# A Swin block on one core: the MLP's rows turned by 32x32 blocks on VectorE and spread by 12 small transfers a unit, in place of TensorE transposes

## What is computed

```python
win = windows of 8x8 pixels of x rolled by (-4, -4)      # (4096, 64, 96)
h = layernorm(win, ln1)
q, k, v = h @ wq + bq, h @ wk + bk, h @ wv + bv          # 3 heads of 32
o = softmax(q k^T / sqrt(32)) v
win = win + o @ wo + bo
h2 = layernorm(win, ln2)
win = win + gelu(h2 @ w1 + b1) @ w2 + b2                 # 96 -> 384 -> 96
result = the windows put back and rolled by (4, 4)
```

## Time and profile before

| | |
|---|---|
| median of 3 runs | 5439.2 us (5439.17 to 5441.29) |
| the profiled execution, its own time | 5443.8 us |
| its span, first to last instruction | 5442.0 us |
| share of the span: PE, DVE, ACT, POOL busy | 95%, 77%, 69%, 57% |
| one batch, from one attention stretch's start to the next | 335 us |

### The profile page before, as it was taken

The page is one execution under the profiler, slowest core; times in us unless marked ns, Lnnn a source line. Parts: engine busy times, 40 slices in busy tenths (PEclk is TensorE's granted clock), DMA queues, the critical chain, the costliest instruction groups (busy, mean ns, idle before and its releaser), DMA issues.

```text
span 5442.0 us, 275140 instructions
## 1 busy us (share of the span) xinstructions
PE 5176.5 (95%) x105172; PEld 4395.4 (81%) x105172; DVE 4179.8 (77%) x9862; ACT 3741.6 (69%) x7758; POOL 3083.7 (57%) x3053
## 2 busy tenths in 40 slices
PE   6999999999999999999999999999999999999999
PEld 4887888878788787888878888788887888878888
DVE  6968768687686877869778697786977869688696
ACT  6839568495784957749477594875938659396693
POOL 5645646466464655646556466464664646556464
PEclk8999999999999999999999999999999999999999
DMA  3011020110201102010120201202011020110201
GB/s 98 3 44 48 27 68 6 47 42 27 68 9 51 36 30 65 11 57 27 33 62 15 61 19 36 59 16 66 13 38 57 19 70 6 41 54 22 73 3 44
DMA packets 92300, 213.96 MB, mean 39 GB/s; under 512 B 22058, under 2 KB 26379, under 8 KB 91851
## 3 DMA queue, kind: packets, MB, share of 16 engines
q1 hardware_dynamic: 91848, 208.20, 13.0%
q10 hardware_dynamic: 2, 0.00, 0.0%
HBM read 107.45 MB, written 100.66 MB: 38 GB/s over the span
## 4 chain that ended last, share of the span: by engine, by line
PE 88%; issue 5%; DVE 5%; SPq 1%; ACT 1%; POOL 0%; DVEq 0%; ACTq 0%; DMA 0%; POOLq 0%
PE psum L585 20%; PE psum L599 19%; PE psum L462 12%; PE psum L430 8%; PE psum L508 6%; PE psum L477 6%; PE psum L494 6%; PE psum L538 5%; PE psum L524 5%; DVE row_max L828 1%; DVE stats L807 1%; DVE stream L857 1%; SPq L251 1%; DVE probs L835 0%; DVE prob_sum L843 0%
## 5 line engine op out<-in xcount | busy, mean ns | idle before, releaser
L297 POOL TENSOR_TENSOR probs<-probs,prob_inv 128x512 f32<-128x512 f32 x771 | 783.1, 1044 | 1496.7 <-DVE prob_inv L851 1496.6
L857 DVE TENSOR_TENSOR stream<-stream,psum 128x384 f32 x1024 | 562.4, 553 | 850.3 <-PE psum L599 760.8
L736 ACT ACTIVATE gelu_odd<-psum 128x512 f32<-128x512 f32 x768 | 459.9, 599 | 732.7 <-PE psum L585 676.9
L736 ACT ACTIVATE gelu_even<-psum 128x512 f32<-128x512 f32 x768 | 459.6, 598 | 682.8 <-PE psum L585 627.1
L376 POOL TENSOR_TENSOR stream<-stream,b_all 128x768 f32 x256 | 493.2, 1931 | 612.4 <-DVE normed L877 584.8
L659 ACT ACTIVATE normed<-stream,shift,rstd 128x96 f32 (+1 forms) x2072 | 770.7, 461 | 43.9 <-POOL shift L345 23.2
L807 DVE BATCH_NORM_STATS2 stats<-stream (+2 forms) x4224 | 725.9, 243 | 57.1 <-DVE stream L857 38.9
L336 POOL TENSOR_TENSOR rstd<-variance,minus_half 128x32 f32<-128x32 f32 (+3 forms) x181 | 747.7, 4131 | 14.2
L304 POOL TENSOR_TENSOR hT<-hT_upper,hT_lower 96x1024 f32<-96x1024 f32 x258 | 613.6, 2378 | 22.8 <-issue 15.6
L828 DVE TENSOR_REDUCE row_max<-psum 128x8 f32<-128x512 f32 x771 | 523.8, 679 | 131.7 <-PE psum L494 116.6
L843 DVE TENSOR_REDUCE prob_sum<-probs 128x8 f32<-128x512 f32 x771 | 497.8, 679 | 109.1 <-ACT probs L693 109.1
(11 more groups left out here) (86 smaller groups left out, 10635.3 us busy)
## 6 DMA issues: line engine op xcount, KB each, us to landing
stream<-in_x SPq DMA_DIRECT2D x272, 192.0 KB
out<-stream SPq DMA_DIRECT2D x256, 192.0 KB
stream<-in_x SPq DMA_DIRECT2D x272, 180.0 KB
out<-stream SPq DMA_DIRECT2D x256, 180.0 KB
stream<-in_x SPq DMA_DIRECT2D x544, 6.0 KB
out<-stream SPq DMA_DIRECT2D x512, 6.0 KB
gelu_odd<-in_L_conv_w SPq DMA_DIRECT2D x1, 144.0 KB
w_w<-in_L_conv_w SPq DMA_DIRECT2D x1, 144.0 KB
```

The lines of the kernel that those rows point to most:

```text
L297: nc.gpsimd.tensor_tensor(block_h, block_h, inv, ALU.mult).then_inc(probs_ready, 1)
L736: nc.scalar.activation(gelu[parity][:, j, part * SHARES:(part + 1) * SHARES], psum[:, UP_BANKS[part][j], :], ACT.Gelu).then_inc(gelu_done, 1)
L857: nc.vector.tensor_tensor(part, part, psum[:, banks[g], 0:GROUP], ALU.add).then_inc(added, 1)
```

## The change

The MLP's h2 no longer goes through PE and PSUM.

- **Turning.** `turn_h2` on DVE transposes `normed2` by blocks of 32x32: 4 blocks of tokens x 3 blocks of channels for each of 8 tiles, in one instruction. Each block is turned where it lies, so it stays on its 32 partitions.
- **Spreading.** SP then moves the blocks to the partitions of their channels: 12 transfers a unit (`spread_h2`), each of 32 partitions x 256 values, 32 KB. They count on two semaphores, six transfers each.
- **Halves.** The upper half of `h2T` is made from the spread rows by ACT (`copy_h2T_upper`, two instructions of 96x512), for units 0 and 1 by DVE. The lower half is made by DVE as before, but from SBUF.
- **Buffers.** Turned rows of units 0 to 2 lie in a part of `gelu[1]`, the later ones in `normed1`; spread rows lie in `gelu[0]` (units 0, 1) and then alternately in `probsT` and `oT`, all idle at that time. There is one turned buffer for the units from 3 on: turning a unit waits until the unit before it has been spread.
- **Order of tokens.** Spread rows have the tokens of a tile in another order, so gelu writes its result through a view that puts them back.
- **Three units ahead.** Units 0, 1 and 2 of a batch are normalised by POOL in attention steps 4, 6 and 9, turned by DVE after steps 5, 8 and 11 and spread by SP; DVE makes the halves of units 0 and 1 after steps 6, 7, 9 and 10. Unit 2 is spread once attention of unit 15 has read `probsT`. `statistics1` moves from steps 8 to 10 to steps 2 to 4, and POOL has six `finish` calls in attention instead of four.
- **PE.** `transpose2` is gone. `down` waits for all six gelu tiles at once, where before each of its parts waited for three.

```diff
+            def spread_h2(u, source, raw, freed):
+                wait_apart(sp, h2_turned, u + 1)
+                if freed is not None:
+                    wait_apart(sp, *freed)
+                for tb in range(TBLOCKS):
+                    for cb in range(CBLOCKS):
+                        sp.dma_start(raw[BLOCK * cb:BLOCK * (cb + 1), RUN * tb:RUN * (tb + 1)],
+                                     source[BLOCK * tb:BLOCK * (tb + 1), RUN * cb:RUN * (cb + 1)])\
+                            .then_inc(h2_spread[tb // 2], 16)
+            def spread_late(u, parity):
+                spread_h2(u, turned_late, raw_late[parity], (h2T_copied, 2 * (u - 1)))
             def store_batch(batch_row):
-                with sp.Fori(0, BATCH_ROWS) as r:
+                batch = 2 * batch_row
+                spread_h2(batch, turned_early, raw_early[0], None)
+                spread_h2(batch + 1, turned_early, raw_early[1], None)
+                spread_h2(batch + 2, turned_early, raw_late[0], (pv_done, batch + BATCH))
+                with sp.Fori(0, 6) as r:
                     for half in (0, 1):
+                        spread_late(batch + 2 * r + half + 3, 1 - half)
                         store(batch_row + r, half)
+                spread_late(batch + BATCH - 1, 1)
...
-            def transpose2(u, steady):
-                pe.wait_ge(ln2_ready, u + 1)
-                if steady:
-                    pe.wait_ge(gelu_done, 2 * FCHUNKS * u - FCHUNKS)
-                for g in range(2):
-                    transpose_rows(normed2, T2_BANKS, g, t2_done)
...
+            def mlp_step(u, parity):
+                up(u, parity, 1, True)
+                up(u + 1, 1 - parity, 0, True)
+                down(u, parity, True)
...
+            def copy_h2T_upper(u, parity):
+                for g in range(2):
+                    tokens = slice(g * SHARES, (g + 1) * SHARES)
+                    act.wait_ge(h2_spread[g], 16 * SPREAD_DMAS * (u + 1))
+                    nc.scalar.activation(h2T[parity][0][0:C, tokens], raw_late[parity][:, tokens], ACT.Copy)\
+                        .then_inc(h2T_upper_done, 1)
...
+                gelus(batch, 0, 0)
+                with act.Fori(0, BATCH // 2 - 1) as k:
+                    for odd in (0, 1):
+                        j = 2 * k + odd
+                        gelus(batch + j, odd, 1)
+                        copy_h2T_upper(batch + j + 2, odd)
+                        gelus(batch + j + 1, 1 - odd, 0)
...
+            def turn_h2(u, turned, first):
+                dve.wait_ge(ln2_ready, u + 1)
+                if not first:
+                    for half in h2_spread:
+                        wait_apart(dve, half, 16 * SPREAD_DMAS * u)
+                nc.vector.transpose(turned.rearrange("p (b t i) -> p t b i", b=CBLOCKS, i=BLOCK),
+                                    normed2[:, :, :].rearrange("p t (b i) -> p t b i", i=BLOCK))\
+                    .then_inc(h2_turned, 1)
...
                 def mlp_step(j, parity, row, half):
-                    copy_h2T(batch + j + 1, 1 - parity)
-                    normalise2(batch + j + 2, j + 2)
-                    if row is not None:
-                        statistics1(batch + BATCH + AHEAD + j, AHEAD + j, batch_row + BATCH_ROWS + row, half)
-                    scale2(b, j + 2)
+                    normalise2(batch + j + 3, j + 3)
+                    scale2(b, batch + j + 3, j + 3)
+                    turn_h2(batch + j + 3, turned_late, False)
+                    statistics1(batch + BATCH + AHEAD + j, AHEAD + j, batch_row + BATCH_ROWS + row, half)
+                    copy_h2T_lower(batch + j + 2, parity, raw_late)
                     add_mlp(batch + j)
```

More of the change, by code:

```diff
@@ L589, in up, with down @@
                     last.then_inc(up_done, 1)
[L591 to L600, removed]
[L601 to L616 removed]
+            def down(u, parity, steady):
+                pe.wait_ge(gelu_done, 2 * FCHUNKS * (u + 1))
+                for part in range(2):
+                    if steady:
+                        pe.wait_ge(mlp_added, 2 * u + part)
+                    for t in range(TILES // 2):
+                        c = part * (TILES // 2) + t
+                        for j in range(FCHUNKS):
+                            for side in range(2):
+                                last = nc.tensor.matmul(
+                                    psum[WT * side:WT * (side + 1), DOWN_BANKS[part], t * C:(t + 1) * C],
+                                    gelu[parity][:, j, c * P + WT * side:c * P + WT * (side + 1)], w2_w[:, j, :],
+                                    start=(j == 0), stop=(j == FCHUNKS - 1))
+                    last.then_inc(down_done, 1)
+            def mlp_step(u, parity):
+                up(u, parity, 1, True)
+                up(u + 1, 1 - parity, 0, True)
+                down(u, parity, True)
             for u in range(-AHEAD, 0):
@@ L753, in _ @@
                 nc.scalar.preload_act_table_set("gelu_and_others")
-                with act.Fori(0, BATCH // 2) as k:
-                    for parity in (0, 1):
-                        gelus(batch + 2 * k + parity, parity, 0)
-                        gelus(batch + 2 * k + parity, parity, 1)
+                gelus(batch, 0, 0)
[5 more added lines that the diff above has]
+                        gelus(batch + j + 1, 1 - odd, 0)
+                gelus(batch + BATCH - 2, 0, 1)
+                gelus(batch + BATCH - 1, 1, 0)
+                gelus(batch + BATCH - 1, 1, 1)
         @block.vector
@@ L928, in _, with whole_step @@
                 batch = b * BATCH
-                with dve.Fori(0, 4) as r:
+                def whole_step(s):
+                    attention_step(batch + s, s % 2)
+                    statistics2(batch + s, s)
+                for s in range(2):
+                    whole_step(s)
+                for n in range(AHEAD):
+                    whole_step(2 + n)
+                    statistics1(batch + BATCH + n, n, batch_row + BATCH_ROWS + n // 2, n % 2)
+                whole_step(5)
+                turn_h2(batch, turned_early, True)
+                whole_step(6)
+                copy_h2T_upper(batch, 0)
+                whole_step(7)
+                copy_h2T_lower(batch, 0, raw_early)
+                whole_step(8)
+                turn_h2(batch + 1, turned_early, False)
+                whole_step(9)
+                copy_h2T_upper(batch + 1, 1)
+                whole_step(10)
+                copy_h2T_lower(batch + 1, 1, raw_early)
+                whole_step(11)
+                turn_h2(batch + 2, turned_early, False)
+                with dve.Fori(6, 8) as r:
                     for half in (0, 1):
```

153 lines of the change are left out of this document (78 added, 75 removed).

## The result

| | before | after |
|---|---|---|
| median of 4 runs, us | 5439.2 (5437.2 to 5441.3) | 5930.0 (5921.3 to 5934.8) |
| profiled execution, us (span) | 5443.8 (5442.0) | 5934.8 (5933.0) |
| mean granted clock of TensorE | 0.987 | 0.948 |
| from A to the end of the MLP stretch, mean of 16 | 150.4 | 176.1 |
| from there to the next A, mean of 15 | 185.2 | 190.3 |

After/before is 1.0901, 95% interval 1.0882 to 1.0919: 30.7 us more for each of the 16 batches. The last two lines are worked out from the ends of PE's last `project_out` product (A) and last `down` product of each batch: 25.7 us of the loss lie in the MLP stretch, 5.1 in attention.

What follows compares the result with a forecast made beforehand. PE was taken to bound the kernel, SP's queue the new MLP stretch: 151.05 - 135.2 = 15.85, minus 1.75 in attention, 14.1 us a batch, 226 in 16, giving 5213 us; range 5150 to 5400.

Steps and rivals of the forecast that it cites:

- Slower: Rival, chance 0.16: SP's issues cost what a store's do, I = 8.4, giving 5847 us; decides from a pitch of 0.515.
- I: SP's time to issue the 12 spreading transfers of one unit in the MLP stretch; forecast 5.1 us, ends 4.4 and 5.7.
- the price of an issue: SP's cost for each spreading transfer, taken as 0.415 us, the middle between two kinds of transfer in the earlier trace.
- the bound of 0.47: Upper end of the pitch of SP's 12 issues expected in the profile after, 0.36 to 0.47 us.
- start of unit 4's spreading: SP in the MLP stretch: unit 4 turned at A + 14.4, after add_mlp of unit 0, plus 0.2.
- eleven gaps between spreadings: SP's time between groups of 12 issues, units 4 to 15: six of 4.6 us and five of 2.8.
- Two units take 2I + 7.4, against PE's 16.5: MLP stretch: SP's loop over two units against two PE steps; the queue keeps pace up to I = 4.55 us.
- A + 74.0 + 12 I: End of the MLP stretch if SP's queue bounds; meets PE's A + 133.0 at I = 4.92, 135.2 us with 5.1.
- The PE-bound stretch: MLP stretch if PE bounds it: 133.0 us against 151.05, with steps of 8.24 us, a gain of 18.05 a batch.
- seven insertions: DVE's three turns, two upper and two lower pairs added in attention; forecast to cost 1.75 us a batch.
- the 0.3 us above: Cost to an attention step of one DVE insertion of 1.2 to 1.6 us, taken from steps holding statistics1.
- The bound of 8.1 us a batch: Attention: cost of DVE's added work if none of it is hidden, 3 x 0.97 + 4 x 1.3.

Runs made afterwards that it cites:

- cheap issues: Changed kernel with each of the 12 transfers reading its rows from the input in DRAM instead of the turned tile; output not the reference's; 5467.2 us, ratio 1.0045.
- through DRAM: Changed kernel with turned rows written to DRAM in one transfer and read back in three, early halves in mid-step; 5199.8 us, ratio 0.9550.
- both edits: Changed kernel with six double-size transfers a unit (rows misplaced) and the early halves in the middle of the next attention step; 5198.6 us, ratio 0.9557.
- repeated copies: Version with turned rows going by way of DRAM, each early upper copy made three times and each early lower half twice; 5285.4 us.
- six-issue version: Changed kernel with six transfers of twice the size a unit instead of 12, bytes unchanged, rows misplaced; 5286.0 us, ratio 0.9712.
- moved halves: Changed kernel with DVE's early halves of units 0 and 1 in the middle of the next attention step, behind three subtractions; 5845.7 us, ratio 1.0739.

## Why the prediction was wrong, point by point

It was wrong in sign, with 0.80 on faster. The rival *Slower* is what happened: the queue bounds, and the pitch, 0.633, is past the 0.515 from which it decides. Its reason was another than the one I gave for it: the spreading has no computed patterns, and the same transfers out of DRAM cost 0.42. That its 5847 us comes near 5930 is partly luck: it took I = 8.4, and with the measured 7.6 the same sum gives 74.0 + 91.2 = 165.2 for the stretch and 5693 us in all.

**The step that failed** is the price of an issue: "I take the middle, 0.415, so I = 12 x 0.415 + 0.1 for the wait = 5.1. Ends: 4.4 and 5.7". It interpolated over rows and bytes between rows that all had DRAM at one side; no row before showed a transfer with both sides in SBUF, and the bound of 0.47 did not hold for it. Measured: I = 7.6. Of the 12 x (7.6 - 5.1) = 30.0 us a batch that this costs, 12 x (7.6 - 5.5) = 25 are for both sides in SBUF (5.5 is I with DRAM at one side); the other 5 come from averaging in the pitch of 0.36, where a steady burst out of DRAM has 0.46.

The loss of 30.7 us a batch in place of a gain of 14.1 is a miss of 44.8. By terms, from the mean starts of the spreadings in 14 batches (unit 4 at A + 19.7, unit 15 at A + 148.8, end A + 176.1):

| term | predicted | measured | us a batch |
|---|---|---|---|
| 12 I | 12 x 5.1 | 12 x 7.6 | 30.0 |
| start of unit 4's spreading | A + 14.6 | A + 19.7 | 5.1 |
| eleven gaps between spreadings | 6 x 4.6 + 5 x 2.8 = 41.6 | 129.1 - 11 x 7.6 = 45.5 | 3.9 |
| from the last spreading to the end, I = 7.6 | 25.4 | 27.3 | 1.9 |
| attention | 1.75 | 5.1 | 3.3 |
| stretch before | 151.05 (one) | 150.4 (mean) | 0.6 |

- *Start of the queue.* I computed when unit 4 is turned and took SP to be free. But unit 3's own spreading starts at A + 8.4 and takes an I itself, and a store follows. So the stretch grows with 13 I, not 12. With cheap issues (I = 5.5) unit 4 starts at A + 17.6, with six (3.9) at A + 15.6. Some 1.6 us of the late start are unit 3's subtraction, 2.54 us beside POOL where I took 0.94; no run removed that.
- *Gaps.* The short one is right (2.7). The one behind six stores is 12.9 - 7.6 = 5.3, not 4.6: the waits and register work ahead of and behind the six issues are 0.5 and 0.7 us, where I took 0.45.
- *Tail.* PE had idled for 2.94 us, and its first `up` ran at PEclk 0.56: 3.88 us for 2.2. I had priced the first work after the wait at the full clock.
- *The law of the steady step held, the sum around it did not.* "Two units take 2I + 7.4, against PE's 16.5" gives 22.6 against a measured 23.2 with 12 issues, and for six about 15, below 16.5, where PE does bound. "A + 74.0 + 12 I" falls short by 10.9 us with I = 7.6 (165.2 against 176.1), by the three terms above. For the cheap issues, I = 5.55, it gives 140.6 against 146.8: the start is 3.0 late there, the gaps are 3.8 longer, and the tail is 0.7 shorter.

**The PE-bound stretch** came out at 135.4 in four versions (six issues, through DRAM, both edits, repeated copies), against 133.0. The step is 8.41 in place of 8.24, and 14 x 0.17 = 2.4. The products did not get slower: I had taken too much away. The chain gives the eight transposes 1.01 us, but the first product of `up` starts before they have ended. PE in the kernel before:

```profile
1619.64 0.48 PE L585 MATMUL psum<-h2T_even_upper,w_split_upper 128*128 128x512 f32 x1
...
1623.99 4.18 PE L599 MATMUL psum<-w_w,gelu_even 128*64 128x96 f32 x96
1628.10 1.08 PE L430 MATMUL psum<-ident,normed 128*96 128x128 f32 x8
1628.94 0.48 PE L585 MATMUL psum<-h2T_odd_upper,w_split_upper 128*128 128x512 f32 x1
```

From the first transpose to the first product it is 1628.94 - 1628.10 = 0.84 us (the median of 240). From the first product of `up` to the first of `down` the median of 224 is 4.31 us before and 4.30 through DRAM, and from there on 4.11 in both. So a step loses 0.84 with the transposes, not 1.01.

**Attention.** The seven insertions "by the 0.3 us above" were mis-sized through their lengths, not through the slack. The lower pair was priced by the row of DVE reading PSUM, 0.677; reading two tiles in SBUF beside a POOL operation that reads SBUF it took 2.51. The Trainium skill (SBUF — State Buffer, "Who interferes with whom") states that a DVE instruction with two SBUF inputs contends with a GpSimd instruction that reads SBUF, and that one of them blocks until the other is done; it says the same of a copy in a mode that uses the second port. The traces agree: the slow ones end 0.28 and 0.55 us behind POOL's operation, and the moved ones take 0.68 and 0.42. In which mode the copy runs no trace shows. The bound of 8.1 us a batch held. The slack was as read in the earlier trace rows: about 1.3 us of a step takes an insertion free, and the length beyond it is paid in part. With short pairs the seven insertions cost nothing that can be seen (184.6 and 185.1 us to the next A, against 185.2), where I had forecast 1.75.

**The turn** was right: 0.978 us (208 of them) against 0.97, and the three early ones, 0.96 us each, cost attention nothing. (The 311 ns for a square that the prediction cites are for bf16 values; these are float32.) DVE's idle time before it, 950.8 us in 192 places, ended by a transfer, was the announced sign of a bound queue. **The landing** is 1.8 us from issue, of which 0.6 is the issue: 1.2 after it, as taken. ACT and DVE are not the bound in the stretch, as the six-issue version shows. POOL's and the loads' new places did not make attention longer (184.6 against 185.2, once the halves had moved).

**What I should have given weight.** The rivals ranked the pitch by three rows of DRAM transfers of other shapes. The bounds of an operation that no row shows have to reach to every row of its kind, the store's 0.64 included; it stood outside my range, with 0.16. And at the cheap price the kernel is still 0.45% slower than before, because of the start, the gaps and attention.

## What to carry to other kernels

Work taken off the busiest engine and cut into many small transfers is paid for on the queue that issues them: count issues a step times the price of this kind (0.63 us here for SBUF to SBUF, 0.46 for the same shape out of DRAM), add what else the queue carries in the loop, and compare it with the step. If it does not fit, fewer transfers by way of DRAM mended it here (four in place of 12, together with the moved halves, 5200 us against 5439); a second issuing engine for a quarter of them recovered 397 of the 491 us lost, and the kernel stayed slower than before. And price a DVE operation with two SBUF inputs by what POOL does beside it, not by its PSUM twin.

## What the runs showed of the hardware

- An issue on SP with both sides in SBUF takes 0.58 to 0.65 us for 4 to 128 rows and 384 to 3,072 bytes a row. With one side in DRAM it takes 0.41 to 0.43 for 32 rows of 1,024 B and 96 of 1,536 B, but that price is not flat: 4 rows of 1,536 B take 0.26 to 0.31 in a store, 128 rows of 3,072 B into DRAM rose from 0.35 to 0.94 us from the fourth on in a burst, and a store of 60 rows takes 0.95 where one of 64 takes 0.62.
- The first issue of a burst differs from the rest: 0.33 to 0.37 us with DRAM on one side, 0.55 to 0.74 with SBUF on both.
- ACT and SP issue at the same time with pitches of 0.61 and 0.65 us, SP alone with 0.633.
- DVE's turn by 32x32 blocks of a 128x768 float32 tile takes 0.978 us, about as long as the scaling of the same tile (0.97).
- A DVE copy 96x512 that takes 0.42 us in SBUF alone took 1.8 beside POOL's sum, and a subtraction 2.5 in place of 0.68; one of 128x768 beside POOL's addition took 2.54 in place of 0.95.
- Eight PE transposes that the chain lists with 1.01 us kept PE's next product back by 0.84.
